# Conditional MLP with layer norm on one core: ScalarE's order between batches, first loads, and the last tile

## What is computed

```python
out_nr  = gelu(x @ w1_nr + b1_nr) @ w2_nr + b2_nr              # condition 0
out_tsr = gelu(x @ w1_tsr + b1_tsr) @ w2_tsr + b2_tsr          # condition 1
h = gelu(x @ w1_sr + b1_sr)                                    # condition 2: 512 -> 1024
h = gelu(h @ w2_sr + b2_sr)                                    #              1024 -> 512
out_sr = h @ w3_sr + b3_sr                                     #              512 -> 512
y = x + (the one that the condition picks)
result = (y - mean(y)) * rsqrt(var(y) + 1e-5) * gamma + beta
```

## Time and profile before

| what | value |
|---|---|
| median of 3 runs | 562.02 us |
| profiled execution | 561.57 us |
| its span | 559.8 us |
| TensorE busy | 549.4 us (98%), 2423 matmuls |
| VectorE, ScalarE, GpSimd busy | 48%, 38%, 45% |
| granted TensorE clock, mean | 0.998 of 2.4 GHz |
| DMA moved | 61.27 MB, 109 GB/s on average |

### The profile page before, as it was taken

One profiled execution on the slowest core, in us unless ns is written; L12 is line 12 of the kernel. 1 busy time (PEld: TensorE's weight loads), 2 busy tenths in 40 slices (PEclk: granted clock), 3 DMA queues, 4 the chain that ended last, 5 costly groups with the idle time before them and its releaser, 6 DMA issues. The chain is left out here.

```text
span 559.8 us, 8281 instructions
## 1 busy us (share of the span) xinstructions
PE 549.4 (98%) x2423; PEld 452.4 (81%) x2424; DVE 267.7 (48%) x417; ACT 213.1 (38%) x328; POOL 254.6 (45%) x225
## 2 busy tenths in 40 slices
PE   9999999999999999999999999999999999999994
PEld 6878887888888888888888888888888888888883
DVE  5661174865955856113610468212866105501656
ACT  5451335254253454214421452424255124513351
POOL 0879998575675576300430046700175300430056
PEclk9999999999999999999999999999999999999999
DMA  8875404444353443300330034400144200410032
GB/s 304 337 250 184 152 6 143 154 150 154 111 185 140 160 150 119 106 0 0 116 108 0 0 144 156 150 0 0 75 150 148 77 0 28 146 51 0 0 134 92
DMA packets 26225, 61.27 MB, mean 109 GB/s; under 512 B 3042, under 2 KB 3042, under 8 KB 26082
## 3 DMA queue, kind: packets, MB, share of 16 engines
q1 hardware_dynamic: 26208, 61.10, 31.2%
q10 hardware_dynamic: 2, 0.00, 0.0%
HBM read 44.31 MB, written 16.78 MB: 109 GB/s over the span
## 5 line engine op out<-in xcount | busy, mean ns | idle before, releaser
L456 DVE TENSOR_TENSOR g_lo<-bank,g_hi 128x512 fp32r<-128x512 f32 x112 | 77.4, 691 | 252.8 <-DVEq L117 252.8
L406 ACT ACTIVATE g_hi<-bank,bcol 128x512 fp32r<-128x512 f32 x112 | 77.8, 694 | 161.4 <-ACTq L117 160.2
L596 POOL TENSOR_TENSOR y<-y,row 128x512 f32<-128x512 f32 x64 | 95.2, 1507 | 51.0 <-POOLq L117 50.6
L600 POOL TENSOR_SCALAR var_eps<-mv 128x2 f32<-128x2 f32 x30 | 6.5, 218 | 227.6 <-POOLq L117 227.5
L428 ACT ACTIVATE y<-y,rstd 128x512 f32<-128x512 f32 x63 | 42.2, 717 | 172.0 <-ACTq L117 172.0
L236 PE MATMUL bank<-w_hi,g_hi 128*128 128x512 f32 x256 | 99.8, 390 | 1.2 <-PEq L117 1.2
L238 PE MATMUL bank<-w_hi,g_lo 128*128 128x512 f32 x256 | 99.7, 389 | 0.0
L237 PE MATMUL bank<-w_lo,g_hi 128*128 128x512 f32 x256 | 99.7, 389 | 0.0
L236 PE MATMUL bank<-x_hi,w_hi 128*128 128x512 f32 x240 | 93.5, 390 | 0.0
L237 PE MATMUL bank<-x_lo,w_hi 128*128 128x512 f32 x240 | 93.4, 389 | 0.0
L238 PE MATMUL bank<-x_hi,w_lo 128*128 128x512 f32 x240 | 93.4, 389 | 0.0
(11 more groups left out here) (42 smaller groups left out, 597.2 us busy)
## 6 DMA issues: line engine op xcount, KB each, us to landing
y<-x SPq DMA_DIRECT2D x64, 256.0 KB, 3.6
out<-y SPq DMA_DIRECT2D x64, 256.0 KB, 2.5
stage<-x_t SPq DMA_DIRECT2D x31, 512.0 KB, 3.3
w_raw<-weights SPq DMA_DIRECT2D x17, 512.0 KB, 4.7
row<-rows SPq DMA_DIRECT2D x1, 1280.0 KB, 11.4
stage<-x_t SPq DMA_DIRECT2D x2, 256.0 KB, 3.8
w_raw<-weights SPq DMA_DIRECT2D x2, 256.0 KB, 4.2
cond_sb<-cond ACTq DMA_DIRECT2D x1, 0.1 KB
```

The costliest lines, as they stand in the source:

```text
L406: eng.activation(g_hi[:, slot, :], psum, ACT.Gelu, bias=b)
L456: eng.tensor_tensor(g_lo[:, slot, :], psum, g_hi32[:, slot, :], ALU.subtract).then_inc(s_gs, 1)
L596: eng.tensor_tensor(y[:, t, :], y[:, t, :], row[:, kind, :], ALU.add).then_inc(s_xb, 1)
L600: eng.tensor_scalar(var_eps[:, t:t + n], mv[:, t:t + n, 1], EPS, None, ALU.add).then_inc(s_var, n)
```

## The change

ScalarE no longer scales a batch's tiles 2 and 3 at the end of that batch. From the second batch on it does so in the following batch, after the two Gelus of the first hidden chunk (`normalise_late`); a register counts the batches for that, and the first batch still scales all four tiles at its end. With it the bank releases of tiles 2 and 3 (`s_acc`) move too. SyncE issues the first two row loads of batch 0 ahead of the x halves of batch 1. In the last batch the last tile is centred within its PSUM bank, and finished in two column halves; the first half is stored by SyncE, the second by ScalarE's DMA queue. GpSimd adds beta to the third tile of the last batch in two halves, one before and one after the last 1/standard deviation.

```diff
@@ sync: first loads
+            load_row(0, 0)
+            load_row(0, 1)
             for f in range(2):
                 take(eng, s_stage[f])
                 load_x(x_halves[2 + f], f)
-            for t in range(TT):
-                load_row(0, t)
+            load_row(0, 2)
+            load_row(0, 3)
@@ sync: end
-            for t in range(TT):
-                store(NBATCH - 1, t, s_fin if t < FINISHED_BY_OTHERS_END else s_fin_end)
-            for t in range(TT):
-                take(eng, s_out[t], 16)
+            for t in range(TT - 1):
+                store(NBATCH - 1, t)
+            take(eng, s_fin_end[0])
+            eng.dma_start(out_end[0], y_end[0]).then_inc(s_out[TT - 1], 16)
+            for t in range(TT):
+                take(eng, s_out[t], 32 if t == TT - 1 else 16)
@@ scalar
-            def body(kind, read_next, last):
+            def normalise(t):
+                take(eng, s_v)
+                eng.sem_inc(s_acc, 1)
+                take(eng, s_rstd)
+                eng.activation(y[:, t, :], y[:, t, :], ACT.Copy, scale=rstd[:, t:t + 1]).then_inc(s_n, 1)
+
+            def body(kind, read_next, b):
                 read_next()
                 for j in range(n_hidden(kind)):
                     gelu(bank[hidden_bank(kind, j)][:, :], j % 4, B1[kind] + j)
+                    if j == 0:
+                        normalise_late(b)
...
-                for t in range(FINISHED_BY_OTHERS_END if last else TT):
-                    take(eng, s_v)
-                    if kind != NONE:
-                        eng.sem_inc(s_acc, 1)
-                    take(eng, s_rstd)
-                    eng.activation(y[:, t, :], y[:, t, :], ACT.Copy, scale=rstd[:, t:t + 1]).then_inc(s_n, 1)
+                normalise(0)
+                normalise(1)
+                if b is END:
+                    normalise(2)
+                    return
+                with eng.If_cmp(turn, 0, "IS_EQ"):
+                    normalise(2)
+                    normalise(3)
+                eng.reg_add(turn, turn, 1)
+
+            def normalise_late(b):
+                if b is END:
+                    normalise(2)
+                    normalise(3)
+                else:
+                    with eng.If_cmp(turn, 2, "IS_GE"):
+                        normalise(2)
+                        normalise(3)
...
+            take(eng, s_fin_end[1])
+            eng.dma_start(out_end[1], y_end[1]).then_inc(s_out[TT - 1], 16)
@@ vector: last tile
+                for h in range(2):
+                    eng.scalar_tensor_tensor(out=y_end[h], in0=made_in(kind, 3)[:, halves[h]], scalar=rstd[:, 3:4], in1=row[:, R_BETA, halves[h]],
+                                             op0=ALU.mult, op1=ALU.add).then_inc(s_fin_end[h], 1)
...
-                centre(kind, 3, s_v_end)
-                finish(kind, 3)
+                eng.scalar_tensor_tensor(out=made_in(kind, 3), in0=made_in(kind, 3), scalar=mv[:, 3, 0:1], in1=row[:, R_GAMMA, :],
+                                         op0=ALU.subtract, op1=ALU.mult).then_inc(s_v_end, 1)
+                finish(kind)
@@ gpsimd: end
-            shift(2)
+            take(eng, s_n)
+            shift_half(0).then_inc(s_half, 1)
             deviation_end(3, s_rstd_end)
+            take(eng, s_half)
+            shift_half(1).then_inc(s_fin, 1)
```

More of the change, by code:

```diff
@@ L35 @@
 ORDER_SR = [(j, t) for j in range(2) for t in range(TT)] + [(j, t) for t in range(TT) for j in (2, 3)]
-FINISHED_BY_OTHERS_END = 3
+FINISHED_BY_OTHERS_END = TT - 1
 N_WARM, N_WARM_SHORT = 9, 14
@@ L111, in conditional_mlp @@
         s_n = sem("s_n")
-        s_fin, s_fin_end = sem("s_fin"), sem("s_fin_end")
+        s_half = sem("s_half")
+        s_fin, s_fin_end = sem("s_fin"), [sem(f"s_fin_end{h}") for h in range(2)]
         s_out = [sem(f"s_out{t}") for t in range(TT)]
@@ L159, in pair @@
             return slice(first, first + 2)
+        halves = [slice(0, H // 2), slice(H // 2, H)]
+        out_end = [out.rearrange("b (p c) h -> b p c h", c=TT)[NBATCH - 1, :, TT - 1, h] for h in halves]
+        y_end = [y[:, TT - 1, h] for h in halves]
         block = ctx.enter_context(nc.Block())
@@ L175, in tile_of, with store @@
                 return dram[bass.ds(b, 1), :, t, :].rearrange("a p h -> p (a h)")
-            def store(b, t, finished=s_fin):
-                take(eng, finished)
+            def store(b, t):
+                take(eng, s_fin)
                 eng.dma_start(tile_of(out_rows, b, t), y[:, t, :]).then_inc(s_out[t], 16)
@@ L322, in step @@
                 if kind == NONE:
+                    take(eng, s_acc, 4)
                     read_next()
@@ L416, in body @@
                     gelu(bank[hidden_bank(kind, j)][:, :], j % 4, B1[kind] + j)
+                    if j == 0:
+                        normalise_late(b)
+                if kind == NONE:
+                    normalise_late(b)
                 if kind == SR:
@@ L419, in body @@
                         gelu(bank[i][:, :], i, B2[SR] + i, (1, 1, 2, 0)[i])
-                if not last:
+                if b is not END:
                     split_x(0)
                     split_x(1)
-                for t in range(FINISHED_BY_OTHERS_END if last else TT):
-                    take(eng, s_v)
-                    if kind != NONE:
-                        eng.sem_inc(s_acc, 1)
-                    take(eng, s_rstd)
-                    eng.activation(y[:, t, :], y[:, t, :], ACT.Copy, scale=rstd[:, t:t + 1]).then_inc(s_n, 1)
+                normalise(0)
[7 more added lines that the diff above has]
+                eng.reg_add(turn, turn, 1)
+            END = NBATCH - 1
+            turn = eng.alloc_register("turn_Activation")
+            eng.reg_mov(turn, 0)
+            def normalise_late(b):
[6 more added lines that the diff above has]
+                        normalise(3)
             eng.dma_start(cond_sb[:, 0:NBATCH], cond.rearrange("(a b) -> a b", a=1)).then_inc(s_cond, 16)
@@ L448, in _ @@
             with eng.Fori(0, NBATCH - 1) as b:
-                batch(eng, cond_of, b, lambda kind, read_next: body(kind, read_next, False))
-            batch(eng, cond_of, NBATCH - 1, lambda kind, read_next: body(kind, read_next, True))
+                batch(eng, cond_of, b, lambda kind, read_next: body(kind, read_next, b))
+            batch(eng, cond_of, END, lambda kind, read_next: body(kind, read_next, END))
+            take(eng, s_fin_end[1])
+            eng.dma_start(out_end[1], y_end[1]).then_inc(s_out[TT - 1], 16)
         @block.vector
@@ L488, in variance, with finish @@
                 eng.tensor_scalar(var_eps[:, t:t + 1], mv[:, t:t + 1, 1], EPS, None, ALU.add).then_inc(s_var, 1)
-            def finish(kind, t):
+            def finish(kind):
                 take(eng, s_v_end)
                 take(eng, s_rstd_end)
-                eng.scalar_tensor_tensor(out=y[:, t, :], in0=y[:, t, :], scalar=rstd[:, t:t + 1], in1=row[:, R_BETA, :],
-                                         op0=ALU.mult, op1=ALU.add).then_inc(s_fin_end, 1)
+                for h in range(2):
+                    eng.scalar_tensor_tensor(out=y_end[h], in0=made_in(kind, 3)[:, halves[h]], scalar=rstd[:, 3:4], in1=row[:, R_BETA, halves[h]],
+                                             op0=ALU.mult, op1=ALU.add).then_inc(s_fin_end[h], 1)
             def hidden(kind):
@@ L614, in deviations_of_all, with shift_half @@
                     deviations(t, 2)
+            def shift_half(h):
+                return eng.tensor_tensor(y[:, 2, halves[h]], y[:, 2, halves[h]], row[:, R_BETA, halves[h]], ALU.add)
             def shift_all():
```

## The result

The changed kernel takes 572.5 us (median of 5 runs, 571.81 to 573.11); the kernel before, run beside it, 562.02 us (561.69 to 562.25). The ratio is 1.0188, 95% interval 1.0174 to 1.0202. The forecast was 566.8 us, range 564.6 to 568.6: slower, as forecast, but by 10.5 us instead of 4.8, and outside the range.

A forecast was written before the change was run, and what follows sets the result against it. The prediction took TensorE's stream to bound the kernel. Its terms, 4.3 + 0.15 + 0.15 + 0.2 = +4.8 us on the profiled 561.57, gave 566.4, plus 0.45 to the median: 566.8 us, range 564.6 to 568.6.

The forecast's parts named there:

- Part 1, NR batches: Batches 3 to 6 and 12: two late scalings delay ScalarE's chain; 0.86 us lost each, +4.3 us (bounds 4.0 and 5.0).
- The chain: From an NR batch's first Gelu, ScalarE feeds VectorE and that TensorE; slack 0.51 us, pushed back by 1.23 us.
- the two pieces: In each NR batch the 0.86 us loss comes at chunk 1 and again at chunk 3.
- Part 1, batches 1 and 2: At most 0.2 us won at batch 2, against 0.3 there and 0.1 at batch 1; together +0.1 to +0.2 us.
- rival (d): Later stores and row loads on SyncE, or fetched ScalarE code, delay each NR batch; 570.5 us, chance 0.09.
- In batch 2 the last layer starts 1 us earlier and stalls at chunk 1: Sign expected in the profile after: two scalings instead of four precede batch 2's first chunk, the other two precede chunk 1.
- Part 2: Row loads first, batch 0: additions start at 21.9, statistics 0.24 us later; +0.15 us (bounds 0 and +0.3).
- Part 3: At the end, tile 2's later store and both halves of tile 3 queue at DMA; +0.2 us (bounds -0.3 and +0.4).
- What bounds the kernel: TensorE's stream, busy for 98% of the span, with two waits only, 1.2 us and 0.8 us.
- (a): Faster: the scalings cost the chain nothing and each stall shrinks; 560.5 us, chance 0.04.
- (b): No change: slack larger than 0.51 us, or late scalings fall before the Gelu; 562.0 to 562.8 us, chance 0.07.

The follow-up runs named there:

- nr_ahead: no_none with the late scalings placed ahead of the first Gelu in NR batches; 563.27 us, ratio 1.0027.
- one_late: no_none with tile 2 scaled at the end of its own batch, so only tile 3 is late; 564.84 us, ratio 1.0054.
- code_only: The kernel before, order untouched, with never-reached code for ScalarE added inside the loop; 564.37 us, ratio 1.0051.
- code_behind: The kernel before with the same never-reached code as code_only, but in the last batch's body behind the loop; 561.88 us, ratio 1.0000.
- no_none: The changed kernel with ScalarE's body for a fourth condition, which doesn't occur in these inputs, left empty; 567.91 us, ratio 1.0111.
- loads_only: The kernel before with only row loads 0 and 1 moved ahead of the x halves; 562.20 us, ratio 1.0008.
- tail_halves: The kernel before with the last tile in halves on two queues, GpSimd's third-tile shift kept whole ahead of the last power; 561.51 us, ratio 0.9996.
- late_only: The kernel before with only ScalarE's late scalings of tiles 2 and 3; 571.39 us, ratio 1.0177.
- pool_reorder: The kernel before with GpSimd computing batch 1's deviations among the last weight splits instead of behind them; 560.39 us, ratio 0.9974.

## Why the prediction was wrong, and where it was right

**Part 1, NR batches: right.** +0.95 us each against 0.86 forecast, 4.75 against 4.3, within the bounds of 4.0 to 5.0. The chain, the two pieces and the places are as forecast, and nr_ahead and one_late bear them out. The 0.09 too little is about the 0.08 us of a second restart: TensorE stops twice in each of these batches, and the step counted its restart once.

**Part 1, batches 1 and 2: here the prediction failed**, at the words "I take 0.3 of that here and 0.1 at batch 1 for the register addition and branch (bounds 0 and 0.5)". Both the value and the bound come from the 0.56 us that ScalarE spends between batches before, a loop of the old size. What a larger loop body does at the loop's end was no term of the sum; code that has to be fetched stood in rival (d), for each NR batch and without a price from a row. The hole comes once, at the first pass, and costs 3.3 us of ScalarE's time. The second thing missed is what follows from a long wait: 2.3 us lost to half clock. The span grew by 10.9 us where the sum had 4.8. Of the 6.1 between them, 3.34 + 2.3 = 5.6 are these two; the rest is +0.45 in the NR batches, +0.4 at the end, +0.3 up to batch 2 and -0.7 in batch 2. That the code in the loop makes the hole is shown by code_only (hole without any reordering), code_behind (same code elsewhere, no hole) and no_none (same reordering with less code, no hole). That ScalarE stands there for a fetch of code is the likeliest reading, not shown: in after four packets of 8 KB start between 34 and 41 us, in the kernels of the table without a hole three, but the trace doesn't say which engine each is for. The four take 2.05 us together (1.6% of 16 engines' 8 us), some 0.5 each, so one packet more doesn't account for the length of the hole either. Also open is why the hole is 2.2 us longer than usual in code_only and 3.3 in after, with the loop's end at the same place.

The Trainium skill, Advanced Engine Details and Errata, section "ISA Cache", gives the engines other than TensorE 32 KB for instructions, in two lines of 16 KB or 256 instructions. The runs don't agree with these figures taken alone: by them, an estimate, the whole program of code_only would fit, 343 instructions against 2 x 256, and yet the hole is there with the loop's end at the 229th instruction and not at the 193rd; and the packets are of 8 KB. Where in a line the program starts is shown by no run.

**Batch 2 itself** is -0.63 us, where +0.1 to +0.2 with batch 1 was forecast. That is no gain of the new order: with the hole gone (no_none) it is +0.13. GpSimd, the cause of that wait, used batch 1's delay. The mark "In batch 2 the last layer starts 1 us earlier and stalls at chunk 1" is seen undisturbed in no_none: there it starts 11.28 us into the batch instead of 12.28, and stalls at chunk 1 for 0.8 us. In after it starts with no wait at all, by batch 1's delay, and stalls for 0.58 us.

**Part 2: the mechanism right, the size not told.** Forecast +0.15 with statistics 0.24 us later, at most 0.3; in the profile after they are 0.46 later, since the additions start at 22.12 and not at 21.9, and the loads alone give 1.0008 (0.9999, 1.0018). The additions alternate with the x splits as in batch 3: 5.73 us from the first addition to the first statistics, 27.85 - 22.12, the very number of the earlier trace rows; in loads_only it is 28.04 - 22.31, the same.

**Part 3: mis-sized.** Forecast +0.2, measured +0.61 of tail in after (bound was +0.4) and 1.0016 alone. The places are right: the finish starts 4.12 us after the last matmul's start instead of 4.30, and tile 2's store is issued 4.67 us after it instead of 3.74. The failed step is "from 557.4 the DMA engines have tile 2 and both halves to move, 512 KB at 393 GB/s". With rows of 1 KB among them they move 318 GB/s at a share of 0.99; 512 KB take 1.65 us at that rate instead of 1.33, and the data end 7.2 us after the last matmul (569.4) instead of the 6.67 of the earlier trace rows. That tile 2's late store is what costs is shown by tail_halves, which takes it away; that the rows of 1 KB lower the rate is read from this one stretch.

**What bounds the kernel: right, with a slip.** The waits of TensorE before were not two: a third, of 0.8 us, lies at the very start, before and after alike, and no term of the sum hung on it.

**The rivals.** (a) and (b) are out: the first Gelu of batch 3 starts 8.22 us into the batch, before and after, where TensorE lets it be. (d) named the likely cause, code to be fetched, as one of two, but with the wrong place (each NR batch) and thus the wrong sum; its time, 570.5, is nearer than the forecast's by accident. The five NR batches show no hole.

## What to carry to other kernels

Work put into a chain of producer and consumer costs its full length once the chain's slack is used up, so measure that slack at its last link before reordering, and put extra work where the engine waits for its input anyway (nr_ahead). Count an edit's instructions too, not only its time: in a loop with several branches of which some never run, code grows in every branch, and the hole that this brings at the first pass can cost more than the operations. And price a wait of TensorE together with the clock that it may lose behind it; at an end of the kernel, ask what each earlier store still has in flight when the last one is issued.

## What the runs showed of the hardware

- The hole at the first pass of ScalarE's grown loop, with the weight loads running at some 240 GB/s: the idle time before the Gelu grew from 0.56 to 2.79 us (code_only), 3.50 (late_only, which has part 1 alone) and 3.90 (after). It happens once in a run.
- Waits of TensorE and what came behind them, beyond its step of 0.227 us: 1.0 us (before), 1.35 (no_none) and 1.85 (nr_ahead, in batch 2) left the clock at 2.4 GHz; 2.26 (code_only) and 3.42 (late_only) were followed by 3.4 us at 1.2 GHz, 4.64 (after) by 6.8. In after the clock fell before TensorE went on, in code_only 0.5 us after it and in late_only 1.4. The window of late_only:

```profile
43.60:47.00 3.40, 3.40 (x10) 2.62 (x9) 1.38 (x2) 1.20 (x3) 3.22 (x3) 0.51 0.83 257
```

- The first layer of batch 0 starts anywhere from 5.27 to 6.86 us in the profiles, in kernels that are the same there. It hardly reaches the end: batch 2 starts at 82.76 us with a start of 5.29 and at 83.10 with one of 6.86 (pool_reorder), because the wait at batch 1 shrinks with it (batch 1 takes 55.60 us and 54.40). So single profiles should be compared from a mark behind such a wait.
